# Small inputs joined to the first key tile's transfer, targets in two halves

## The reference

```python
B, L, D = (512, 200, 64)
scaler = jnp.float32(D) ** 0.5
q = target_key @ W_target.T
k = jnp.einsum('bld,ed->ble', item_keys, W_item)
v = jnp.einsum('bld,ed->ble', item_values, W_value)
scores = jnp.einsum('bd,bld->bl', q, k) / scaler
scores = scores + -100000000.0 * (1.0 - mask.astype(scores.dtype))
w = jax.nn.softmax(scores, axis=1)
return jnp.einsum('bl,bld->bd', w, v)
```

## Time and profile before

| | us |
|---|---|
| median of 3 runs | 136.29 |
| lowest, highest | 136.19, 137.0 |
| the profiled execution | 136.88 |
| its span, first to last instruction | 135.0 |
| TensorE busy in it | 74.4 |
| VectorE, ScalarE, GpSimd busy | 20.1, 7.8, 7.5 |

### The profile page before, as it was taken

How to read it: one execution, slowest core, us unless ns; L and a number is a source line. 1 busy time by engine, 2 the same in 40 slices (tenths; PEclk the granted TensorE clock), 3 DMA queues, 4 the chain that set the end, 5 groups by cost and what they waited for, 6 DMA issues and landing times.

```text
span 135.0 us, 1401 instructions
## 1 busy us (share of the span) xinstructions
PE 74.4 (55%) x590; PEld 22.9 (17%) x590; DVE 20.1 (15%) x57; ACT 7.8 (6%) x26; POOL 7.5 (6%) x24
## 2 busy tenths in 40 slices
PE   0002399379384663539670572629770582728981
PEld 0000233022020211212120111212120121211170
DVE  6000000520005000330005000330005000340050
ACT  0300000110000000210000000120000000020000
POOL 7910000000000000010000000010000000010000
PEclk9999999955959599955999689965899689965799
DMA  5999999999999999999999999999999999899700
GB/s 137 452 393 402 394 430 409 438 426 449 404 448 410 440 443 426 426 431 449 381 478 394 455 411 457 402 456 412 418 463 394 470 403 464 387 403 422 280 10 10
DMA packets 3765, 53.24 MB, mean 394 GB/s; under 512 B 1072, under 2 KB 1136, under 8 KB 1584
## 3 DMA queue, kind: packets, MB, share of 16 engines
q1 hardware_dynamic: 2736, 52.43, 91.8%
q10 hardware_dynamic: 1024, 0.74, 1.7%
HBM read 53.04 MB, written 0.13 MB: 394 GB/s over the span
## 4 chain that ended last, share of the span: by engine, by line
DMA 76%; PE 21%; SPq 1%; issue 1%; DVE 0%; ACT 0%; DVEq 0%
DMA value_a<-values_a 76%; PE ps_context L479 11%; PE ps_context L484 4%; PE ps_context L488 3%; PE ps_late L522 1%; PE ps_late L514 1%; SPq L185 1%; PE ps_small L542 0%; PE ps_late L507 0%; PE ps_small L532 0%; ACT result L294 0%; DVE context_late L400 0%; DVE context_t L408 0%; DVEq L407 0%; DVEq L399 0%
## 5 line engine op out<-in xcount | busy, mean ns | idle before, releaser
L451 PE MATMUL ps_scores<-key_ring,sta_query 128*32 128x400 f32 x256 | 29.1, 607 | 22.7 <-DMA key_ring<-keys 22.2
L479 PE MATMUL ps_context<-value_a,sta_full 128*32 128x512 f32 x64 | 14.6, 1060 | 6.6 <-DMA value_a<-values_a 6.6
L451 PEld LDWEIGHTS ps_scores<-key_ring,sta_query 128*32 128x32 f32 x256 | 8.8, 130 | 41.3 <-DMA key_ring<-keys 25.5
L390 DVE TENSOR_TENSOR context_slots<-ps_context,in_octet 128x512 f32<-128x512 f32 x4 | 2.8, 692 | 42.0 <-PE ps_context L501 35.3
L344 DVE SCALAR_TENSOR_TENSOR second_biased<-ps_scores,in_pair,mask_bias 128x200 f32<-128x200 f32 x4 | 1.7, 426 | 39.7 <-PE ps_scores L451 39.7
L240 POOL COPY half_twice<-expd 128x128 f32<-128x128 f32 x4 | 1.4, 351 | 110.5 <-ACT expd L269 110.5
L496 PE MATMUL ps_context<-value_b,sta_half 128*32 128x512 f32 x24 | 4.1, 757 | 6.1 <-DMA value_b<-values_b 6.1
L501 PE MATMUL ps_context<-value_b,sta_full 128*32 128x512 f32 x48 | 6.5, 666 | 0.0
L430 PE MATMUL ps_small<-w_query_sb 64*64 64x128 f32 x2 | 0.7, 444 | 10.3 <-DMA w_query_sb<-w_query 10.3
L484 PE MATMUL ps_context<-value_a,sta_eighth 128*32 128x512 f32 (+1 forms) x32 | 6.2, 852 | 0.0
L461 PE MATMUL ps_turn_full<-ident,expd 128*128 128x128 f32 x4 | 1.3, 323 | 7.0 <-ACT expd L269 7.0
(11 more groups left out here) (63 smaller groups left out, 42.1 us busy)
## 6 DMA issues: line engine op xcount, KB each, us to landing
key_ring<-keys SPq DMA_DIRECT2D x8, 3200.0 KB, 26.3
value_a<-values_a SPq DMA_DIRECT2D x4, 3328.0 KB, 25.2
value_b<-values_b SPq DMA_DIRECT2D x3, 3072.0 KB, 27.6
value_b<-values_b SPq DMA_DIRECT2D x1, 1280.0 KB, 25.5
value_b<-values_b SPq DMA_DIRECT2D x1, 1024.0 KB, 22.7
value_b<-values_b SPq DMA_DIRECT2D x1, 512.0 KB, 26.2
mask_sb<-mask_rows ACTq DMA_DIRECT2D x1, 400.0 KB, 21.6
value_b<-values_b SPq DMA_DIRECT2D x1, 256.0 KB, 26.4
```

The lines of the kernel that those rows point to most:

```text
L390: nc.vector.tensor_tensor(context_slots[:], ps_context[:].rearrange("p (x d) -> p x d", x=OCT), in_octet[:].unsqueeze(2).to_broadcast([P, ...
L451: last = nc.tensor.matmul(ps_scores[g * GU:(g + 1) * GU, 0:QB], window(sta_query, g, s * QUADS_T + k), key_ring[:, s, c:c + QB], start=s = ...
L479: nc.tensor.matmul(ps_context[g * GU:(g + 1) * GU, :], window(sta_full, g, k), value_a[:, c:c + OB], start=k == 0, stop=False)
```

## The change

The five inputs `w_query`, `targets`, `w_value_cols`, `mask_rows` and the first key tile become one input, `first`, of 128 rows: 6,400 columns of keys, then W_target (64), W_item (64), half of the targets (256), W_value^T (64) and the mask (800), 7,648 columns in all. Rows 0 to 63 hold the targets of users 0 to 255, rows 64 to 127 those of users 256 to 511; the weights stand in both halves. SyncE loads it with one transfer in the place of the first key tile; the four issues of ScalarE are gone. In SBUF it lies behind the room for the second key tile, and later first tiles of a block land in its first 6,400 columns only, so the small inputs stay where they are.

TensorE makes the product of the weights twice, on each half of the partitions, and the queries of blocks 0 and 1 from the lower half, those of blocks 2 and 3 from the upper; the second set of queries is two products instead of one. The conversion of the mask and the product with W_value read the same tile.

```diff
-        key_ring = sb("key_ring", [P, NT, KCOLS])
+        key_room = sb("key_room", [P, KCOLS + FIRST])
+        first_tile = key_room[:, KCOLS:]
+        key_slot = (key_room[:, KCOLS:2 * KCOLS], key_room[:, 0:KCOLS])
+        w_target = first_tile[:, W_TARGET:W_ITEM]
+        w_item = first_tile[:, W_ITEM:TARGETS]
+        targets = first_tile[:, TARGETS:W_VALUE]
+        w_value_twice = first_tile[:, W_VALUE:MASK]
+        mask = first_tile[:, MASK:FIRST].bitcast(mybir.dt.int32)
...
-        w_both = sb("w_both", [D, 2 * D])
+        w_both = sb("w_both", [P, 2 * D])
...
-        ps_query = psum("ps_query", [P, B])
+        ps_query = [psum(f"ps_query{h}", [P, B // 2]) for h in range(2)]
...
-                    sp.dma_start(key_ring[:, s, :], keys[n * NT + s]).then_inc(s_key[s], 16)
+                    if n == 0 and s == 0:
+                        sp.dma_start(first_tile, first).then_inc(s_key[s], 16)
+                    else:
+                        sp.dma_start(key_slot[s], keys[n * NT + s - 1]).then_inc(s_key[s], 16)
...
-            act.dma_start(w_query_sb[:], w_query).then_inc(s_w_query, 16)
-            act.dma_start(targets_sb[:], targets).then_inc(s_targets, 16)
-            act.dma_start(mask_sb[:], mask_rows).then_inc(s_mask, 16)
-            act.dma_start(w_value_twice[:], w_value_cols).then_inc(s_w_value, 16)
-
-            act.wait_ge(s_both, 1)
+            act.wait_ge(s_both, 2)
...
-            dve.wait_ge(s_mask, 16)
-            nc.vector.tensor_scalar(mask_bias[:], mask_sb[:], -1.0, MASKED, ALU.add, ALU.mult).then_inc(s_mask_bias, 1)
+            dve.wait_ge(s_key[0], 16)
+            nc.vector.tensor_scalar(mask_bias[:].rearrange("p n l -> p (n l)"), mask, -1.0, MASKED, ALU.add, ALU.mult).then_inc(s_mask_bias, 1)
...
-            pe.wait_ge(s_w_query, 16)
-            nc.tensor.matmul(ps_w_both, w_query_sb[:, 0, :],
-                             w_query_sb[:, 1, :].unsqueeze(1).to_broadcast([D, 2, D]),
-                             start=True, stop=True).then_inc(s_both, 1)
+            pe.wait_ge(s_key[0], 16)
+            for h in range(2):
+                rows = slice(h * D, (h + 1) * D)
+                nc.tensor.matmul(ps_w_both[rows, :], w_target[rows, :],
+                                 w_item[rows, :].unsqueeze(1).to_broadcast([D, 2, D]),
+                                 start=True, stop=True).then_inc(s_both, 1)
             pe.wait_ge(s_both_copied, 1)
-            pe.wait_ge(s_targets, 16)
-            nc.tensor.matmul(ps_query[:, 0:P], w_both[:], targets_sb[:, 0:P], start=True, stop=True) \
+            nc.tensor.matmul(ps_query[0][:, 0:P], w_both[0:D, :], targets[0:D, 0:P], start=True, stop=True) \
                 .then_inc(s_query, 1)
+
+            def other_queries():
+                nc.tensor.matmul(ps_query[0][:, P:2 * P], w_both[0:D, :], targets[0:D, P:2 * P], start=True, stop=True)
+                nc.tensor.matmul(ps_query[1][:, :], w_both[D:P, :], targets[D:P, :], start=True, stop=True) \
+                    .then_inc(s_query, 1)
...
                     if n == 0 and s == 0:
-                        nc.tensor.matmul(ps_query[:, P:B], w_both[:], targets_sb[:, P:B], start=True, stop=True) \
-                            .then_inc(s_query, 1)
+                        other_queries()
```

More of the change, by code:

```diff
@@ L42, with masked_attention_kernel @@
 MASKED = 1.0e8
-def masked_attention_kernel(nc, w_query, targets, w_value_cols, mask_rows, keys, values_a, values_b, out):
+def masked_attention_kernel(nc, first, keys, values_a, values_b, out):
     B, D = out.shape
-    L = mask_rows.shape[2]
+    L = FULL + HALF + EIGHTH
     NBLK = B // P
@@ L53, in masked_attention_kernel @@
     KCOLS = QUADS_T * GRP * QB
-    assert FULL + HALF + EIGHTH == L and 2 * D == P and B % P == 0
+    W_TARGET = KCOLS
+    W_ITEM = W_TARGET + D
+    TARGETS = W_ITEM + D
+    W_VALUE = TARGETS + B // 2
+    MASK = W_VALUE + D
+    FIRST = MASK + NBLK * L
+    assert tuple(first.shape) == (P, FIRST)
+    assert 2 * D == P and B == 4 * P
     A_HALF = OB
@@ L75, in sem @@
             return ctx.enter_context(nc.semaphore(name))
-        key_ring = sb("key_ring", [P, NT, KCOLS])
+        key_room = sb("key_room", [P, KCOLS + FIRST])
[6 more added lines that the diff above has]
+        mask = first_tile[:, MASK:FIRST].bitcast(mybir.dt.int32)
         value_a = sb("value_a", [P, A_COLS])
         value_b = sb("value_b", [P, B_COLS])
-        w_query_sb = sb("w_query_sb", [D, 2, D])
-        targets_sb = sb("targets_sb", [D, B])
-        w_value_twice = sb("w_value_twice", [P, D])
-        w_both = sb("w_both", [D, 2 * D])
-        mask_sb = sb("mask_sb", [P, NBLK, L], mask_rows.dtype)
+        w_both = sb("w_both", [P, 2 * D])
         mask_bias = sb("mask_bias", [P, NBLK, L])
@@ L126, in masked_attention_kernel @@
         ps_eighth_t = ps_turn_rest[:, P:2 * P]
-        ps_w_both = ps_small[0:D, 256:256 + 2 * D]
+        ps_w_both = ps_small[:, 256:256 + 2 * D]
         ps_context_t = ps_small[:, 0:P]
         ps_project = ps_small[:, P:P + D]
[L131 to L134, removed]
         s_key = [sem(f"s_key{s}") for s in range(NT)]
@@ L259, in place_odd_queries @@
                     act.wait_ge(s_key_used, NT * n)
-                users = ps_query[D:P, n * P:(n + 1) * P].rearrange("p (g i b e) -> p g i b e", g=GRP, b=2, e=2)
+                users = ps_query[n // 2][D:P, n % 2 * P:(n % 2 + 1) * P].rearrange("p (g i b e) -> p g i b e", g=GRP, b=2, e=2)
                 nc.scalar.copy(sta_query[D:P, :, :, 1:4:2], users[:, :, :, :, 1]).then_inc(s_sta_odd, 1)
@@ L333, in place_even_queries @@
                     dve.wait_ge(s_key_used, NT * n)
-                users = ps_query[0:D, n * P:(n + 1) * P].rearrange("p (g i b e) -> p g i b e", g=GRP, b=2, e=2)
+                users = ps_query[n // 2][0:D, n % 2 * P:(n % 2 + 1) * P].rearrange("p (g i b e) -> p g i b e", g=GRP, b=2, e=2)
                 nc.vector.tensor_copy(sta_query[0:D, :, :, 0:4:2], users[:, :, :, :, 0]).then_inc(s_sta_even, 1)
@@ L452, in score @@
                             ps_scores[g * GU:(g + 1) * GU, 0:QB], window(sta_query, g, s * QUADS_T + k),
-                            key_ring[:, s, c:c + QB], start=s == 0 and k == 0,
+                            key_slot[s][:, c:c + QB], start=s == 0 and k == 0,
                             stop=s == NT - 1 and k == QUADS_T - 1)
@@ L535, in project @@
             def project(n):
-                if n == 0:
-                    pe.wait_ge(s_w_value, 16)
-                else:
+                if n > 0:
                     pe.wait_ge(s_result, n)
@@ L592 @@
     values_b[NBLK - 1] = np.concatenate([late_half, late_full], axis=1)
-    arrays = {
-        "w_query": np.stack([inputs["L0_rec_W_target"], inputs["L0_rec_W_item"]], axis=1),
-        "targets": target.T,
-        "w_value_cols": np.concatenate([np.asarray(inputs["L0_rec_W_value"]).T] * 2, axis=0),
-        "mask_rows": mask.reshape(NBLK, P, L).transpose(1, 0, 2),
-        "keys": k,
+    halves = np.split(np.asarray(target).T, 2, axis=1)
+    small = np.concatenate([
+        np.concatenate([inputs["L0_rec_W_target"], inputs["L0_rec_W_item"], half_targets,
+                        np.asarray(inputs["L0_rec_W_value"]).T], axis=1) for half_targets in halves], axis=0)
+    mask_rows = np.ascontiguousarray(mask.reshape(NBLK, P, L).transpose(1, 0, 2).reshape(P, NBLK * L))
+    small = np.concatenate([small, mask_rows.view(np.float32)], axis=1)
+    arrays = {
+        "first": np.concatenate([k[0], small], axis=1),
+        "keys": k[1:],
         "values_a": np.concatenate([eighth, half[:, 0], full[:, 0]], axis=2),
```

## The result

| | kernel before | changed kernel |
|---|---|---|
| median, us | 137.07 (136.19 to 137.42, 6 runs) | 135.03 (133.96 to 136.17, 6 runs) |
| the profiled execution, us | 136.88 | 135.22 |
| its span, us | 135.0 | 133.5 |
| TensorE's mean granted clock | 0.848 | 0.834 |

The account below looks back on a forecast made before the run. The prediction took transfer-queue bytes and engine use to bound the kernel up to 121.84 us. Its terms, -1.64 - 0.61 + 1.49 = -0.76 us with the tail at 0, took 136.29 to 135.5 us, range 134.7 to 136.9.

Parts of the forecast that it names:

- The bound: Up to the last L479 at 121.84 us, bytes in the transfer queues and use of the 16 engines set time.
- the cover: First block: sta_full ready at 27.3 to 28.1 us, value_a landing at about 28.0; slack used up to within 0.1.
- (a): Transfer engines up to 28.7 us: removing the packets of the four small loads saves 1.64 us of every engine.
- (b): From 10 to 14 us: the targets' transfer slows rows beside it; removing it saves 0.61 us per engine, bounds 0 and 0.61.
- Rival 1: Nothing is gained: the slow stretch from 10 to 14 us comes with the second key tile and stays; 136.1 us, chance 0.14.
- The added columns: First transfer grows by 1,248 columns, 0.639 MB, costing 1.49 us at the steady price, at most 1.81.
- the sum: Transfer engines over the whole run: -1.64 - 0.61 + 1.49 = -0.76 us, with later distances between blocks unchanged.
- The tail: Behind the last L479: low-clock stretch between 4.11 and 5.29 us, moving the end by -0.14 to +0.46 us; taken as 0.
- The head: Start of compute: first tile lands at 13.1 us, weights' half products take at most 1.38, first score at 16.0.
- rival 2: Faster by over 1%: an instruction-queue packet falls on an engine that is ahead, gaining 1.3 us more; 134.2 us, chance 0.07.
- rival 3: Slower by over 1%: instruction-queue packets pile up on one engine, 1.3 us each; 138.1 us from three on, chance 0.03.

Follow-up runs that it names:

- four spare loads: Changed kernel plus all four old small loads, issued in the old order into tiles nobody reads; ratio 1.009 to the kernel before, 137.69 us.
- with fillers: Extra products nobody needs in the last block; with 22, the kernel before took 135.72 us, the changed kernel 134.44 us.
- with halves: Kernel before, still four loads, with targets as two halves on 128 partitions and query weights in both halves; ratio 0.996.
- three spare loads: Changed kernel plus the old query weights, mask and value matrix loads, without the targets, read by nobody; ratio 1.004 to the kernel before.
- one spare load: Changed kernel plus one unread load of 64 x 2,048, 128 x 1,024 or 128 x 2,048 bytes; ratios 0.996, 0.995, 0.996 to the kernel before.
- the first profile: First profiled execution of the changed kernel, against the kernel before: 135.22 us, span 133.5 us.
- the second: Profile of the changed kernel run again unaltered: span 134.2 us; ratio 0.992 to the kernel before.
- spare targets in halves: Changed kernel plus an unread load of the targets' bytes as 128 partitions x 1,024 bytes; ratio 0.995 to the kernel before.

## Why the prediction was right, and where it was small

**The bound and the cover were right.** Up to the last L491 the transfer engines set the time. The small loads' packets cost what their own length says, and a head whose compute came 4 us later wasn't felt at the end.

**Terms (a) and (b)**: 1.64 + 0.61 = 2.25 us forecast, 2.24 measured for the four loads put back. The inference in (b), from time alone, holds: the cost moved with the targets' transfer and vanished with its form, at 0.54 to 0.63 us by the rows' lengths. Rival 1 has fallen.

**The added columns**: 1.49 forecast. The kernel with four spare loads differs from the kernel before, in what it loads, by the longer first rows alone: 29.38 - 28.03 = 1.35 us at tile 3. The rows themselves took 8 x (1,133 - 949) ns = 1.47 us longer, so the term's size was right; the other 0.12 lies in each engine's first row and in the rows beside the targets, which differ by as much between executions of one kernel. The gain at tile 3 is 0.91, not 0.76.

**What the sum lacked: it let a gain of the first 28 us stay as it is.** From tile 3 to tile 14 the median engine takes 83.57 us in the kernel before, 83.56 with fillers, 83.75 with halves, 83.59 with four and 83.47 with three spare loads; in the changed kernel 83.24 and 83.26, with fillers 83.24 to 83.31, and 83.26 to 83.35 with one spare load. The kernels without the three or four loads pass these tiles about 0.3 us sooner (0.5 against the one with halves). A part is no riddle: packets of the value matrix (0.08 us of each engine), and with halves of the mask too (0.27 in all), still move behind tile 3. The rest, 0.2 to 0.3 us, lies in the rows of the whole stretch: from 36 to 112 us key rows take 952 ns in the mean in all five profiles of the one group and 949 to 951 in the nine of the other, rows of value_a 991 against 987, rows of value_b 916 to 918 against 912 to 916. The term was missing from the sum: -2.25 + 1.35 - 0.3 = -1.2, which is what the pair with fillers measured, though only to half a microsecond. What carries it isn't known. The kernels of the slower group also have seven or eight input arrays in HBM, the others four or five, and their tiles lie at other places in SBUF; no run separated this from the loads, nor was it tried whether engines that run more in step hinder each other.

**The tail** was forecast as unmoved within -0.14 to +0.46. In the first profile it moved by -0.5, in the second by +0.1, because the low stretch was 3.25 us long, below the 4.11 that I had taken as its lower bound from three blocks. A bound from three examples of one execution was too narrow.

**The head** was forecast too late. The first tile could be used at 12.71, not 13.1, and the two half products of the weights took 0.69 us together, not 1.38, so the first score came at 15.05 and not 16.0. sta_full was ready at 25.92, not between 27.3 and 28.1, and the cover, called used up, is 2.13 us wide.

**Rivals 2 and 3**: their mechanism is at work, and the packet records show it. The packets of the instruction queue, of 0.9 to 1.1 us each, pass at 32 to 36, near 64 and near 95 us in every profile. Each falls on one engine, and from then on this engine is behind the median one by about 1.5 us more (1.4 to 1.7 in nearly all cases); it doesn't catch up. In the kernel before, three different engines are hit, and the slowest ends 1.79 us behind at the last value_a. In the changed kernel the first packet puts one engine behind, and the second falls on the engine that was already 0.65 late, which ends at 2.13. That is why L491's distances are 31.40, 30.87 and 30.42 us, and why the last L491 gained 1.01 us where the median engine gained 1.26 at that tile. With the spare targets in halves no packet fell on the engine that was 1.19 late at tile 3; it ends at 1.37, the distances are 30.57, 30.46 and 30.48, and the last L491 started 0.25 us before the changed kernel's although the kernel loads more. So which engine is hit moves the landings by over 1 us between kernels, as rival 2 says, and this did not favour the change. In no profile did two of these packets fall on one engine before the last value_a, as rival 3 needs.

## What to carry to other kernels

Where transfer engines set the time, price a small transfer by what its packets take of an engine and by what they do to the rows beside them, not by its latency; joining it to a large row costs its bytes and saves its packets. Try a wide, short tile on all 128 partitions rather than on 64: here it took 0.6 us less of each engine, but as twice the rows it landed later. And before two kernels that differ by 1% are compared, take the clock of the tail out of play, and look at the median engine's landings beside those of the slowest: here the tail's clock alone made 0.6 us between two executions, and one packet on one engine about 1.5.

## What was not expected of the hardware

- A transfer of 64 partitions x 2,048 bytes made the rows beside it slower, by 0.5 to 0.6 us of each engine for 128 KB (22 to 23 KB per us and engine instead of 27); the same bytes as 128 x 1,024, or 128 x 2,048, did not. The Trainium skill (DMA: Bandwidth & Descriptors, Rules for kernel authors) advises to join small transfers. The runs agree: the four loads cost 2.24 us, and joining them gave back 0.9 of it at tile 3 after the longer rows were paid. But 0.6 of the 2.24 came from the form of one of them.
- Kernels with three or four small loads at the start take 0.2 to 0.3 us more over the next 83 us of the same tiles, in rows that are 2 to 4 ns longer; whether the loads cause it is not shown.
- One packet of the instruction queue, of about 1 us, puts one transfer engine about 1.5 us behind the others to the end of the loads, and each landing waits for the slowest.
- 22 products that nobody needs made the kernel before 0.4% faster (0.1 to 0.6) and the changed one about as much: with them the granted clock is 2.4 GHz behind the last wait, where it was 1.2 for 3.25 to 4.58 us.
